# Slot tables of a routed expert layer: half-precision one-hots made by VectorE and GpSimd in place of single-precision ones made by VectorE and ScalarE

## The reference, cut to what matters

```
gate_probs = softmax(x @ Wg + bg)                  # 2048 tokens, 8 experts
topk_probs, topk_idx = top_k(gate_probs, 2)
topk_probs = topk_probs / sum(topk_probs, -1)      # two weights for each token
h = gelu(x @ W1[e] + b1[e])                        # 256 -> 1024, for each expert
y = h @ W2[e] + b2[e]                              # 1024 -> 256
out = layernorm(x + sum over the two chosen experts of y * weight)
```

## Time and profile before

| | |
|---|---|
| median of three executions | 708.63 us |
| span of the profiled execution | 704.8 us |
| TensorE busy | 610.6 us, 87% |
| VectorE busy | 517.4 us, 73% |
| ScalarE busy | 397.3 us, 56% |
| GpSimd busy | 292.9 us, 42% |
| mean granted TensorE clock | 0.964 of full |

### The profile page before, as it was taken

The page is one execution under the profiler, slowest core; times in us unless marked ns, Lnnn a source line. Parts: engine busy times, 40 slices in busy tenths (PEclk is TensorE's granted clock), DMA queues, the critical chain, the costliest instruction groups (busy, mean ns, idle before and its releaser), DMA issues.

```text
span 704.8 us, 22698 instructions
## 1 busy us (share of the span) xinstructions
PE 610.6 (87%) x8063; PEld 447.7 (64%) x8064; DVE 517.4 (73%) x1106; ACT 397.3 (56%) x847; POOL 292.9 (42%) x245
## 2 busy tenths in 40 slices
PE   2678989999999999999886797899999999999940
PEld 1456756676676667667564556678777777777720
DVE  5797898997786878677677986867666666666635
ACT  4335668767568484866778693554434444444414
POOL 3688574436264641543111012233444444444422
PEclk9789999999999999999999997999999999999985
DMA  8435253240322304304344045122222222222226
GB/s 276 151 103 151 78 166 91 63 121 6 111 69 72 82 1 119 110 21 118 106 121 136 1 119 180 19 32 46 47 47 45 45 45 45 44 45 39 43 40 223
DMA packets 39839, 59.45 MB, mean 84 GB/s; under 512 B 6768, under 2 KB 27504, under 8 KB 39632
## 3 DMA queue, kind: packets, MB, share of 16 engines
q1 hardware_dynamic: 32272, 48.12, 23.3%
q0 software_dynamic: 7488, 10.23, 8.9%
HBM read 34.08 MB, written 11.67 MB: 65 GB/s over the span
## 4 chain that ended last, share of the span: by engine, by line
PE 34%; DVE 11%; DMA 6%; ACT 4%; issue 4%; POOL 2%; ACTq 1%; SPq 1%; DVEq 1%; POOLq 0%
PE bank L1688 6%; PE bank L1690 3%; DVE mxc L1085 3%; DMA x_sb<-x_rows,slot_row 2%; PE scores L1678 2%; PE bank L1678 2%; PE scores L1680 2%; PE scores L1679 2%; PE bank L1292 2%; DMA acc_rows<-x,slot_row 2%; PE bank L1680 2%; PE bank L1679 2%; POOL acc_rows L627 1%; ACT probs L742 1%; PE scores L1343 1%
## 5 line engine op out<-in xcount | busy, mean ns | idle before, releaser
L742 ACT ACTIVATE probs<-scores 128x768 f32<-128x768 f32 (+1 forms) x128 | 114.3, 918 | 51.0 <-PE scores L1349 40.2
L627 POOL DMA_INDIRECT acc_rows<-x,slot_row x39 | 65.2, 1671 | 132.7 <-DVE x L1198 129.8
L1688 PE MATMUL bank<-w_sb,wp 128*128 x312 | 109.9, 380 | 1.9 <-DVE wp L1185 1.9
L1085 DVE TENSOR_REDUCE mxc<-scores 128x4 f32<-128x1024 f32 x64 | 76.5, 1217 | 20.4 <-PE scores L1363 19.8
L1690 PE MATMUL bank<-w_sb,wp 128*128 x312 | 85.1, 273 | 0.0
L813 ACT ACTIVATE probs<-scores,b_sb 128x128 f32<-128x128 f32 x160 | 45.5, 368 | 63.3 <-PE scores L1680 63.3
L813 ACT ACTIVATE probs<-bank,b_sb 128x128 f32<-128x128 f32 x152 | 43.4, 370 | 65.6 <-PE bank L1680 65.6
L1183 DVE CAST wp<-probs 128x512 f16<-128x512 f32 x78 | 36.1, 462 | 60.3 <-ACT probs L813 59.8
L1050 DVE TENSOR_REDUCE mx<-scores 128x6 f32<-128x768 f32 x64 | 59.8, 950 | 15.7 <-PE scores L1331 15.2
L1678 PE MATMUL scores<-xT,w_sb 128*128 128x128 f16 x320 | 61.2, 223 | 2.2 <-DVE xT L909 1.2
L1679 PE MATMUL scores<-xT,w_sb 128*128 128x128 f16 x320 | 61.2, 223 | 0.0
(11 more groups left out here) (267 smaller groups left out, 1712.1 us busy)
## 6 DMA issues: line engine op xcount, KB each, us to landing
w_sb<-w_sb SPq DMA_DIRECT2D x192, 64.0 KB, 2.4
wstage<-in_w_exp SPq DMA_DIRECT2D x16, 512.0 KB
w_sb<-in_w_exp SPq DMA_DIRECT2D x8, 512.0 KB, 5.3
wp<-in_w_exp SPq DMA_DIRECT2D x8, 512.0 KB, 4.2
x_sb<-in_x_by_feature SPq DMA_DIRECT2D x8, 256.0 KB, 3.5
ctx_raw<-in_ctx SPq DMA_DIRECT2D x8, 256.0 KB, 3.1
x_res<-in_x SPq DMA_DIRECT2D x8, 256.0 KB, 3.5
x_rows<-x SPq DMA_DIRECT2D x8, 256.0 KB, 3.1
```

Of the source, the lines that this page charges most:

```text
L627: nc.gpsimd.indirect_dma_start(out=acc_rows[:, :], out_offset=bass.IndirectOffsetOnAxis(ap=slot_row[:, n:n + 1], axis=0), in_=yb[n % 2], i ...
L742: nc.scalar.activation(probs[:, 2 * (k % 4):2 * (k % 4) + 2, 0:cols], ps_p[pair[u, k, b]][:, :, 0:cols], ACT.Exp, scale=(SELF_SCALE, CROSS ...
L1085: nc.vector.tensor_reduce(mxc[:, 2 * k:2 * k + 2, :], ps_p[pair[u, k, b]][:, :, :].rearrange("p h (a k) -> p h a k", a=2), axis=AX.X, op=A ...
L1688: mm(o[:, 0:2 * D], ah[:, u, f, :], weights(e, at, 2 * D), start=(f == 0), stop=(f == FC - 1), skip_group_check=True)
```

## The change

All matrices become half precision. The columns 0 to 127 are copied to half precision once (`lane16`). The weights are scaled by 2^14 and split in a high and a low half-precision part, so the values have three blocks of 128 columns (token number, high, low) in place of two. The value matrices are no longer made by multiplying a one-hot matrix: `slot_values` makes each by one instruction that compares and multiplies, three for each t and choice. The two one-hot roles are joined in one matrix for each choice, `oh_row`, that stands as the stationary operand. VectorE makes all four matrices for each t and choice in the early group; in the late group it makes the one-hot, and GpSimd makes the three value matrices. ScalarE has no part in it any more. In the late group one t, not two, goes with an expert tile, for the tiles 2 to 7, so the final table is made after tile 8 instead of tile 6, and the calculation of the tiles' experts is cut in three parts.

```diff
-onehots = swaps[:, :].rearrange("p (s n) -> p s n", s=2)
-oh_lane, oh_row = [onehots[:, :, i * 2 * P:(i + 1) * 2 * P].rearrange("p s (c l) -> p s c l", c=2) for i in range(2)]
-oh_vals = onehots[:, :, 4 * P:8 * P].rearrange("p s (c a l) -> p s c a l", c=2, a=2)
+gate16 = swaps[:, 0:9 * P].bitcast(F16)
+oh_row = gate16[:, 0:4 * P].rearrange("p (s c l) -> p s c l", s=2, c=2)
+oh_vals = gate16[:, 4 * P:16 * P].rearrange("p (s c a l) -> p s c a l", s=2, c=2, a=3)
+lane16 = gate16[:, 16 * P:17 * P]
+weight_high = sb("weight_high", [P, 2, NT], F16)
+weight_low = sb("weight_low", [P, 2, NT])
...
+
+def slot_values(engine, t, c):
+
+    for a, value in enumerate((tab[:, C_TOK1 + t:C_TOK1 + t + 1], rs1[:, 4 + c, t:t + 1], weight_low[:, c, t:t + 1])):
+        last = engine.tensor_scalar(oh_vals[:, t % 2, c, a, :], lane16, rs1[:, c, t:t + 1], value, ALU.is_equal, ALU.mult)
+    return last
...
+    def late_values(t):
+        pool.wait_ge(v_key, 2)
+        pool.wait_ge(pe_slot, 2 * (t - 1))
+        for c in range(2):
+            last = slot_values(nc.gpsimd, t, c)
+        last.then_inc(p_oh, 1)
+
...
             pool.wait_ge(v_rows, 2)
         if n and n + AHEAD - 1 < N_TILES:
             gather(n + AHEAD - 1)
+        if n == 0:
+            late_values(GATE[1][1])
+        if n < NT - GATE[1][1] - 1:
+            late_values(GATE[1][1] + n + 1)
         scatter(n)
     pool.wait_ge(sc_st, 16 * N_TILES)
     for k, (t0, t1) in enumerate(LAST):
...
-
-    def gate_values(t):
-        act_e.wait_ge(v_oh, t + 1)
-        nc.scalar.activation(oh_vals[:, t % 2, :, 0, :], oh_row[:, t % 2, :, :], ACT.Identity,
-                             scale=tab[:, C_TOK1 + t:C_TOK1 + t + 1])
-        for c in range(2):
-            last = nc.scalar.activation(oh_vals[:, t % 2, c, 1, :], oh_row[:, t % 2, c, :], ACT.Identity,
-                                        scale=rs1[:, 4 + c, t:t + 1])
-        last.then_inc(a_oh, 1)
...
-        link(nc.vector.tensor_tensor(rs1[:, 4:6, at], rs1[:, 2:4, at], rs1[:, 6:7, at].broadcast_to([P, 2, t1 - t0]), ALU.mult))
+        link(nc.vector.scalar_tensor_tensor(rs1[:, 4:6, at], rs1[:, 2:4, at], G_SCALE,
+                                            rs1[:, 6:7, at].broadcast_to([P, 2, t1 - t0]), ALU.mult, ALU.mult))
+        link(nc.vector.tensor_copy(weight_high[:, :, at], rs1[:, 4:6, at]))
+        link(nc.vector.tensor_tensor(weight_low[:, :, at], rs1[:, 4:6, at], weight_high[:, :, at], ALU.subtract))
...
-    def gate_onehots(t):
+    def gate_onehots(g, t):
             dve.wait_ge(pe_slot, 2 * (t - 1))
-        lanes = tab[:, C_LANE:C_LANE + P].unsqueeze(1).broadcast_to([P, 2, P])
-        for o, i in ((oh_lane, 2), (oh_row, 0)):
-            last = nc.vector.tensor_tensor(o[:, t % 2, :, :], lanes,
-                                           rs1[:, i:i + 2, t].unsqueeze(2).broadcast_to([P, 2, P]), ALU.is_equal)
+        for c in range(2):
+            last = nc.vector.tensor_scalar(oh_row[:, t % 2, c, :], lane16, rs1[:, 2 + c, t:t + 1], None, ALU.is_equal)
+            if g == 0:
+                last = slot_values(nc.vector, t, c)
     def count_tiles(count, tiles, scratch):
...
             weigh(n - 1, (n - 1) % 2, 16 * (n - 2) if n > 2 else None)
         if n == 0:
             gate_slots(*GATE[1])
-        elif n in (1, 2, 3):
-            gate_onehots(GATE[1][1] + 2 * (n - 1))
-            gate_onehots(GATE[1][1] + 2 * (n - 1) + 1)
-        elif n == 4:
-            gate_late_tiles()
-        elif n == 5:
+        elif n <= NT - GATE[1][1]:
+            gate_onehots(1, GATE[1][1] + n - 1)
+        elif n == NT - GATE[1][1] + 1:
             dve.wait_ge(pe_slot, 2 * NT)
             nc.vector.tensor_tensor(slots_all, ps_slots[1], slots_kept, ALU.add).then_inc(v_S, 1)
-        elif n == 6:
+        elif n == NT - GATE[1][1] + 2:
             gate_late_rows()
+        if n in (2, 4, 6):
+            gate_late_tiles(n // 2 - 1)
     dve.wait_ge(v_te, 2)
     dve.wait_ge(v_rows, 2)
     with dve.Fori(0, (N_TILES - 2 - FIRST) // 2) as j:
...
-        pe.wait_ge(a_oh, t + 1)
+        pe.wait_ge(v_oh, t + 1)
+        if g:
+            pe.wait_ge(p_oh, t - first + 1)
         for c in range(2):
-            mm(ps_slots[g], oh_lane[:, t % 2, c, :], oh_vals[:, t % 2, c, :, :].rearrange("p a l -> p (a l)"),
-               start=(t == first and c == 0), stop=(t == (last or first + 1) and c == 1)).then_inc(pe_slot, 1)
+            rows, values = oh_row[:, t % 2, c, :], oh_vals[:, t % 2, c, :, :].rearrange("p a l -> p (a l)")
+            done = t == (last or first + 1) and c == 1
+            mm(ps_slots[g], rows, values[:, 0:2 * P], start=(t == first and c == 0), stop=False, skip_group_check=True)
+            mm(ps_slots[g][:, P:2 * P], rows, values[:, 2 * P:3 * P], start=False, stop=done,
+               skip_group_check=True).then_inc(pe_slot, 1)
     def gate_table(g, slots, i0, i1):
         pe.wait_ge(v_S, SEEN + g)
...
         if n == 0:
             gate_ranks(*GATE[1])
-        elif n in (2, 3, 4):
-            for t in range(GATE[1][1] + 2 * (n - 2), GATE[1][1] + 2 * (n - 1)):
-                gate_scatter(1, t, GATE[1][1], NT - 1)
-        elif n == 6:
+        elif 2 <= n <= NT - GATE[1][1] + 1:
+            gate_scatter(1, GATE[1][1] + n - 2, GATE[1][1], NT - 1)
+        elif n == NT - GATE[1][1] + 2:
             gate_table(1, slots_all, FIRST, N_TILES)
     with pe.Fori(0, (N_TILES - 2 - FIRST) // 2) as j:
         for u in range(2):
```

50 lines of the change are left out of this document (25 added, 25 removed), and 2 rows, old and new, of the table UNITS.

## The result

The changed kernel takes 728.88 us (median of 4 runs, 727.51 to 730.19) against 708.13 us for the kernel before (4 runs): a ratio of 1.0305, with an interval from 1.0279 to 1.0332. I had predicted 713.6 us, with 718.5 us as the upper end. The direction was right, the size was not, and 728.9 us lies outside the range.

A forecast was written before the change was run, and what follows sets the result against it. VectorE was taken to bound the early stretch, TensorE the expert tiles. Early +10.0 and late -5.0 us made +5.0 on the 704.8 us span, 709.8, plus 3.8 to the median: 713.6 us, range 704.5 to 718.5.

The forecast's parts named there:

- What bounds the early stretch: Before the expert tiles, VectorE is the bound; its lateness at 417.72 us passes to the expert layer's start.
- Early group, VectorE: 80 added instructions, 0.165 us apart with one pointer, 0.225 with two, replace 20 comparisons: 16.8 against 6.7 us, +10.1.
- rivals 1 and 2: Early VectorE instructions are cheaper: pointers free, 704.9 us, chance 0.2; or the casts' 0.14 us spacing, 707.7 us, chance 0.12.
- rival 4: VectorE's early stream of sixteen instructions does not overlap at all: +16.3 us for it, 719.5 us in all, chance 0.05.
- the right row: Early VectorE spacing was built on rows L1198 and L877, nearest in form because both carry pointers.
- Early group, other engines given nothing: TensorE's 10.0 us of products (3.3 come back) and ScalarE's 10.36 us of values go, priced at no gain.
- Late group, TensorE: In expert tiles, three gate stops of 2.78 us go, six t return at 0.33 us each: -6.3 us.
- GpSimd's term: From the fourth tile on, transpositions run into the gathers by some tenths each: +1.3 us, 0 to 4.
- Late group, GpSimd: GpSimd's late value instructions take 0.3 us each, six for a t 1.8 us, ahead of scatter and gather.
- just covered: GpSimd's six late values end at 456.2 us, before the scatter that started at 456.71 us.
- The upper bound of my term: Without cover, GpSimd's late values take 0.67 us each, 4.0 us for six; scatter and gather 1.7 us late.
- Rival 3: GpSimd and VectorE hold each other up on SBUF; late gain shrinks to -1.5 us, 717.1 us, chance 0.1.

The follow-up runs named there:

- e7: e1 without the low part of the weights and its product in the early group: 710.34 us, ratio 1.0024.
- e4: Kernel before, with a bench of value-instruction forms on GpSimd, VectorE, then both, behind its end; its total time means nothing; GpSimd's value form takes 0.78 us alone.
- e12: e5 with a half-precision early group: one-hots on VectorE, two values on ScalarE, the low part on GpSimd: 706.05 us, ratio 0.9976.
- e5: Changed kernel with the early group of before; late token numbers on GpSimd, the other two late values on VectorE: 706.37 us, ratio 0.9975.
- e1: Changed kernel with the late group's values made by VectorE instead of GpSimd: 716.38 us, ratio 1.0117.
- e8: Changed kernel with GpSimd's late value instructions cut to 16 columns, so it times the layer but does not compute it: 718.24 us, ratio 1.0114.
- e9: e1 with the low part of the weights in the early group made by GpSimd instead of VectorE: 712.15 us, ratio 1.0054.
- e10: e8 with GpSimd's late values moved behind later gathers, so none stands ahead of tile 0's scatter: 723.32 us, ratio 1.0208.

## Why the prediction was right or wrong

**What bounds the early stretch: right in the main.** VectorE's added work is nearly all passed on: 9.5 us more work and 9.1 us more time in one pair of profiles, 9.3 and 7.6 us by the means, and e7 takes 4.4 away and gets 3.9 back. It is not quite one for one. The likely reason, argued and not tested, is that VectorE was not the whole chain before: between 405 and 417.72 us the chain went through ScalarE's values too.

**Early group, VectorE: right.** Spacing 0.165 and 0.222 us, a pair 3.34 us. For the sum of +10.0 us the medians gave 7.8 and 8.1, and the stretch from the first one-hot to the first tile 7.6 (mean of five profiles against six). The size was some 2 us too high: by the same means VectorE's busy time grew by 9.3 us instead of 10.1, its idle time fell by 1.6 us (8.1 to 6.5) instead of 1.0, and I had added 0.3 for collisions. The cheap forms of rivals 1 and 2 and rival 4's stream without overlap are refuted by the spacing. A form without pointers does come every 0.10 us (e4), so it was the pointers that spoke for the right row.

**Early group, other engines given nothing: right for TensorE.** e12 gives the same relief to TensorE and gains nothing that can be measured. ScalarE's relief was not tested by itself.

**Late group, TensorE: right as a mechanism, 2.2 us too large.** The three stops are gone. I gave -6.3 us for that, which leaves 35.7 us for tiles 2 to 8 (36.9 with GpSimd's term); where GpSimd keeps up they take 37.88 us (e5), -4.1. I had said that VectorE would not be late here. In e5 the first matmul of tiles 4, 6 and 8 starts 0.25 to 0.40 us after the last product instead of 0.06, and in e1, with all values on VectorE, 0.84 to 0.96 us, after VectorE's copy of the tokens. e5's median gained only 1.8 us of the 4.1; in its profile 1.3 us are lost again from tile 8 to tile 12 (24.77 us against 23.51), and I don't know where the rest is.

**Late group, GpSimd: wrong, and this is nearly the whole miss.** The step that failed is the size of the value instruction, "I take 0.3, six for a t make 1.8 us", from a fill and a quarter of a two-tensor subtraction. It is 0.78 us alone and 0.89 us on average over the 36 in the changed kernel, so six take 5.3 us. By the same count "just covered" would have held with 0.3 us: the twelve values would end 3.6 us after 457.83 us, before scatter 0 is due. No run shows that, since the shortest instruction tried (e8, 0.54 us on average) is not yet covered. With 0.89, twelve values fill the time to 469.14 us, and the cycle is 8.3 us against 5.7. The upper bound of my term, 0.67 us for each, was below the truth too, and was then priced as a single delay of 1.7 us: in a queue whose cycle is longer than the tile the delay grows with each tile. e8 gives 10.6 of the 12.5 us back by the length alone. The prediction was 15.3 us too low. The late half is off by 16.4 us (+11.4 for -5.0): 14.2 of it is GpSimd's term (53.34 less e5's 37.88 is +15.5, for my +1.3) and 2.2 TensorE's. The early half was some 2 us too high, and the two together nearly give the miss. Of the 15.5 us, 12.5 are TensorE's waits for gathers and some 3 its longer busy time at the lower clock that follows such waits; that second part had no term in the sum.

**The wait that I did not price.** I named what stands behind the wait for the product, but not that the first values wait for the slots, ahead of scatter 0. That held GpSimd for 7.02 us. By itself it costs nothing (e5 has it too, with its scatter 0 at 454.25 us, 0.5 us after the transposition); with long instructions behind it, it does.

**Rival 3: half right, as a side effect.** GpSimd's instruction is lengthened from 0.78 to 1.8 us where VectorE casts and subtracts without a pause (e4). In the changed kernel that is met only now and then: 0.89 us on average, of which 0.78 is its own. VectorE, which the rival feared for, was not held up (e9).

## What to carry to other kernels

Before work is given to an "idle" engine, add up that engine's whole cycle (its new instructions, the DMAs that it issues, the starts between them) and compare it with the cycle of the loop. Below it the work is free, above it the excess is paid in every round: here 5.0 us for a tile was free (e5: 1.9 of values, 1.6 and 1.0 of DMAs, 0.5 of starts), 7.1 and 8.3 were not, with tiles of 5.7 to 6.3 us. Price an instruction on GpSimd from a row of its own form, or measure it: a fill and a two-tensor row divided by four missed it by a factor of 2.6. And when a queue is late, moving work behind its transfers can put it ahead of a consumer that has less in hand. Two warnings on reading: a mean over a row of instructions hides that only some of them had company (1.06 us over the twelve of e4 are 1.8 and 0.78), and a wait for several semaphores is named after the event that came last, which need not be the one it waited for (e10).
